# A GRU with 16 experts behind it: new states by one scan over pairs, 1 - z on GpSimd, fewer experts inside the recurrence

## The reference

```python
def cell(h, x):
    gi = x @ W_ih + b_ih
    gh = h @ W_hh + b_hh
    r = sigmoid(i_r + h_r)
    z = sigmoid(i_z + h_z)
    n = tanh(i_n + r * h_n)
    return (1.0 - z) * n + z * h          # the new state
S = softmax(xf @ router_w + router_b)     # xf: the 4096 states, 16 experts
G, idx = top_k(S.T, 256)
out = xf[idx] @ expert_w + expert_b
y[idx] += G * out
result = x + y
```

## Time and profile before

| | |
|---|---|
| time, median of 3 | 1116.22 us (1114.98 to 1118.48) |
| profiled execution | 1120.15 us, span 1118.0 us |
| TensorE busy | 1099.6 us, 98% of the span |
| VectorE busy | 836.9 us, 75% |
| ScalarE busy | 407.2 us, 36% |
| GpSimd busy | 7.0 us, 1% |
| mean granted TensorE clock | 0.995 |
| chain that ended last | TensorE 94%, VectorE 3%, DMA 1%, no named cause 1% |

### The profile page before, as it was taken

One profiled execution on the slowest core, in us unless ns is written; L12 is line 12 of the kernel. 1 busy time (PEld: TensorE's weight loads), 2 busy tenths in 40 slices (PEclk: granted clock), 3 DMA queues, 4 the chain that ended last, 5 costly groups with the idle time before them and its releaser, 6 DMA issues.

```text
span 1118.0 us, 61876 instructions
## 1 busy us (share of the span) xinstructions
PE 1099.6 (98%) x27307; PEld 904.6 (81%) x27307; DVE 836.9 (75%) x4504; ACT 407.2 (36%) x1618; POOL 7.0 (1%) x31
## 2 busy tenths in 40 slices
PE   8999999999999999999999999999999999999898
PEld 5778888888888888888888888888888888888772
DVE  5777777777777777777777777777777777776786
ACT  2333333343333333333433433333433334333340
POOL 2000000000000000000000000000000000000000
PEclk9999999999999999999999999999999999999999
DMA  6311111001111111001100000000000000001318
GB/s 250 88 22 22 23 22 23 12 15 21 22 23 22 23 22 23 7 19 22 23 13 14 13 13 13 8 9 13 13 13 13 13 13 4 4 3 52 87 31 274
DMA packets 80258, 36.85 MB, mean 33 GB/s; under 512 B 69987, under 2 KB 69987, under 8 KB 79990
## 3 DMA queue, kind: packets, MB, share of 16 engines
q1 hardware_dynamic: 77648, 28.66, 10.7%
q10 hardware_dynamic: 2342, 4.24, 1.1%
HBM read 24.49 MB, written 8.39 MB: 29 GB/s over the span
## 4 chain that ended last, share of the span: by engine, by line
PE 94%; DVE 3%; DMA 1%; issue 1%; SPq 0%; ACT 0%; DVEq 0%
PE gates L567 59%; PE gates L504 25%; PE ffn_ps L610 5%; PE gates L610 4%; DMA whh<-in_L_cond_W_hh 1%; PE log_ps L619 1%; DVE wih L908 0%; DVE u L794 0%; PE log_ps L691 0%; SPq L275 0%; ACT th L396 0%; DVE zT L801 0%; DVE tok L819 0%; SPq L278 0%; DVE z_h L806 0%
## 5 line engine op out<-in xcount | busy, mean ns | idle before, releaser
L567 PE MATMUL gates<-whh,tok 128*16 128x192 f32 x16384 | 714.0, 326 | 4.9 <-DVE tok L819 2.5
L567 PEld LDWEIGHTS gates<-whh,tok 128*16 128x16 f32 x16384 | 558.9, 124 | 111.2 <-DVE tok L819 4.6
L396 ACT ACTIVATE th<-gates 128x128 f32<-128x128 f32 x512 | 140.2, 274 | 340.9 <-PE gates L567 340.9
L794 DVE SCALAR_TENSOR_TENSOR u<-th,gates 128x64 f32<-128x64 f32 x512 | 113.4, 221 | 198.8 <-ACT th L396 198.8
L401 ACT ACTIVATE n_t<-v 128x64 f32<-128x64 f32 x512 | 131.6, 257 | 277.5 <-DVE v L798 277.5
L504 PE MATMUL gates<-wih,xS 128*32 128x192 f32 x3024 | 146.0, 326 | 0.0
L810 DVE STREAM_TRANSPOSE nT<-n_t 128x64 f32<-128x64 f32 x512 | 123.7, 242 | 0.0
L801 DVE STREAM_TRANSPOSE zT<-th 128x64 f32<-128x64 f32 x512 | 121.5, 237 | 0.0
L798 DVE SCALAR_TENSOR_TENSOR v<-u,gates 128x64 f32<-128x64 f32 x512 | 112.9, 221 | 8.8
L504 PEld LDWEIGHTS gates<-wih,xS 128*32 128x32 f32 x3024 | 98.3, 110 | 22.8
L819 DVE SCALAR_TENSOR_TENSOR tok<-new_n,z_h 128x32 f32<-128x32 f32 x512 | 109.8, 214 | 8.7
(11 more groups left out here) (134 smaller groups left out, 526.8 us busy)
## 6 DMA issues: line engine op xcount, KB each, us to landing
x_in<-in_x SPq DMA_DIRECT2D x248, 32.0 KB, 2.1
xs<-in_x SPq DMA_DIRECT2D x18, 256.0 KB, 3.6
out<-tok SPq DMA_DIRECT2D x16, 256.0 KB, 3.8
out<-tok ACTq DMA_DIRECT2D x16, 256.0 KB, 3.8
wih<-in_L_cond_W_ih SPq DMA_DIRECT2D x4, 768.0 KB, 7.2
whh<-in_L_cond_W_hh SPq DMA_DIRECT2D x4, 768.0 KB, 13.7
whh<-in_x SPq DMA_DIRECT2D x12, 256.0 KB, 5.9
we<-in_L_ffn_expert_w SPq DMA_DIRECT2D x1, 1024.0 KB, 5.2
```

What stands on the lines that cost most here:

```text
L396: nc.scalar.activation(th[a][:, :, :].rearrange("p g c -> p (g c)"), gates[t // S % PAIRS][a][:, R_:HN], ACT.Tanh, scale=0.5).then_inc(th_ ...
L567: mm = nc.tensor.matmul(gates[t // S % PAIRS][a][Q * j:Q * j + rows, R_:GC].rearrange("b (g k c) -> b g k c", g=G, k=KH), columns, by_tile ...
L794: V.scalar_tensor_tensor(u[a][:, :], th[a][:, 0, :], 1.0, ps[a][:, HN:GC], ALU.add, ALU.mult).then_inc(u_ready[a], 1)
```

## The change

VectorE no longer makes new_n and the new state by two instructions in each half. GpSimd makes 0.5 - 0.5 * zT into every second element of `away`; the elements between are 0 for good. `nT` now holds pairs: n from the transpose, and z_h beside it. One scan with multiply and add over the 64 elements of `away` and `nT` (state = away * previous + nT) then gives n at the first of each pair (away is 0 there) and away * n + z_h at the second, which is the new state. States live in a ring of two steps, `states`, from which TensorE takes its columns with a stride of two, and GpSimd copies each into its token tile. half_h is made in two halves. The experts start at step 118, with seven tiles in the loop. Rounds hold ten units, short ones six. Of the 512 units 132 instead of 212 are done by the end of the loop, and 334 instead of 391 when the weights have been gathered; 16 tiles instead of 11 are output from PSUM. `we` is loaded in four pieces at steps 4 to 7, and of the 14 late loads all but the first wait for a search round each.

```diff
-    PAD = P
-    IN_LOOP = 12
+    IN_LOOP = 7
-    FIRST = 18
+    FIRST = 118
-    LAST_UNITS, SOFTMAX_UNITS, ROUND_UNITS, SHORT_UNITS = [3, 6, 6, 6], 28, 9, 4
+    LAST_UNITS, SOFTMAX_UNITS, ROUND_UNITS, SHORT_UNITS = [3, 6, 6, 6], 28, 10, 6
-    PSUM_PLACES = [0, 1, 2, 3, 4, 9, 14, 18, 22, 27, 31]
+    PSUM_PLACES = [0, 1, 2, 3, 5, 7, 10, 12, 14, 17, 19, 21, 24, 26, 28, 31]
...
+        away = [sb(f"away{a}", [P, KH, B, 2]) for a in range(2)]
+        nT = [sb(f"nT{a}", [P, S, KH, B, 2]) for a in range(2)]
+        states = [sb(f"states{a}", [P, (1 + S * KH) * B * 2]) for a in range(2)]
+        state = [states[a][:, B * 2:].rearrange("p (s k b two) -> p s k b two", s=S, k=KH, two=2) for a in range(2)]
...
-            sp.dma_start(we[:, :, :], expert_w.rearrange("(k p) d -> p k d", p=P)).then_inc(ffn_w_loaded, 16)
...
                 load_x(n)
+                if n == 2:
+                    for k in range(K):
+                        sp.wait_ge(h_ready[1], 4 + k)
+                        sp.dma_start(we[:, k, :], expert_w[k * P:(k + 1) * P, :]).then_inc(ffn_w_loaded, 16)
...
             for n in range(XS, NT):
+                if n > XS:
+                    sp.wait_ge(cnt_all, n - XS)
                 load_xs(n)
...
+            for t in range(T):
+                for a in range(2):
+                    pool.wait_ge(zT_ready[a], t + 1)
+                    if t:
+                        pool.wait_ge(h_ready[a], t)
+                    nc.gpsimd.tensor_scalar(away[a][:, :, :, 1], zT[a][:, :, rows], -0.5, 0.5, ALU.mult, ALU.add)\
+                        .then_inc(away_ready[a], 1)
+                for a in range(2):
+                    pool.wait_ge(h_ready[a], t + 1)
+                    nc.gpsimd.tensor_copy(by_chunk[:, a * KH:(a + 1) * KH], state[a][:, (t + 1) % S, :, :, 1]).then_inc(h_kept[a], 1)
...
-                    end = PAD + (t - 1) // TT * D + (kc + 1) * P
-                    columns = tok[:, end - rows * TT + (t - 1) % TT:end:TT]
+                    end = (1 + s * KH + kc % KH + 1) * B * 2
+                    columns = states[kc // KH][:, end - rows * 2 + 1:end:2]
...
-                def take_n(a):
-                    dve.wait_ge(nT_ready[a], t + 1)
-                    V.scalar_tensor_tensor(new_n[a][:, :, :], zT[a][:, :, rows], 1.0, nT[a][:, :, rows],
-                                           ALU.subtract, ALU.mult).then_inc(new_n_ready[a], 1)
...
+                def new_state(a):
+                    dve.wait_ge(nT_ready[a], t + 1)
+                    dve.wait_ge(z_h_ready[a], t + 1)
+                    dve.wait_ge(away_ready[a], t + 1)
+                    if t >= S:
+                        dve.wait_ge(h_kept[a], t - S + 1)
+                    V.tensor_tensor_scan(state[a][:, (t + 1) % S, :, :, :].rearrange("p k b two -> p (k b two)"),
+                                         away[a][:, :, :, :].rearrange("p k b two -> p (k b two)"),
+                                         nT[a][:, s, :, :, :].rearrange("p k b two -> p (k b two)"), 0.0, ALU.mult,
+                                         ALU.add).then_inc(h_ready[a], 1)
```

More of the change, by code:

```diff
@@ L108, in gru_expert_choice_kernel @@
         p7 = sb("p7", [P, HN])
-        tok = sb("tok", [P, PAD + NT * D])
+        tok = sb("tok", [P, NT * D])
         half_h = sb("half_h", [P, K, B])
@@ L117, in gru_expert_choice_kernel @@
         zT = [sb(f"zT{a}", [P, KH, Q]) for a in range(2)]
-        nT = [sb(f"nT{a}", [P, KH, Q]) for a in range(2)]
-        z_h = [sb(f"z_h{a}", [P, KH, B]) for a in range(2)]
-        new_n = [sb(f"new_n{a}", [P, KH, B]) for a in range(2)]
+        away = [sb(f"away{a}", [P, KH, B, 2]) for a in range(2)]
+        nT = [sb(f"nT{a}", [P, S, KH, B, 2]) for a in range(2)]
+        states = [sb(f"states{a}", [P, (1 + S * KH) * B * 2]) for a in range(2)]
+        state = [states[a][:, B * 2:].rearrange("p (s k b two) -> p s k b two", s=S, k=KH, two=2) for a in range(2)]
         def tile(n):
-            return tok[:, PAD + n * D:PAD + (n + 1) * D]
+            return tok[:, n * D:(n + 1) * D]
         x_first = tile(NT - 2)
@@ L131, in gru_expert_choice_kernel @@
         ones = tile(NT - 4)[0:1, P:P + Q]
-        bih, bhh = (tok[0:1, PAD + n * D:PAD + (n + G) * D].rearrange("p (g c) -> p g c", g=G) for n in (NT - 8, NT - 12))
+        bih, bhh = (tok[0:1, n * D:(n + G) * D].rearrange("p (g c) -> p g c", g=G) for n in (NT - 8, NT - 12))
         xs = sb("xs", [P, XS, D])
@@ L234, in gru_expert_choice_kernel @@
         nT_ready = [sem(f"nT_ready{a}") for a in range(2)]
-        new_n_ready = [sem(f"new_n_ready{a}") for a in range(2)]
+        z_h_ready = [sem(f"z_h_ready{a}") for a in range(2)]
+        away_ready = [sem(f"away_ready{a}") for a in range(2)]
+        h_kept = [sem(f"h_kept{a}") for a in range(2)]
         h_ready = [sem(f"h_ready{a}") for a in range(2)]
@@ L330, in _ @@
                                     channel_multiplier=1).then_inc(ident_ready, 1)
-            nc.gpsimd.memset(tok[:, 0:PAD], 0.0).then_inc(pad_cleared, 1)
+            for a in range(2):
+                nc.gpsimd.memset(away[a][:, :, :, :], 0.0)
+                nc.gpsimd.memset(states[a][:, :], 0.0).then_inc(pairs_cleared, 1)
             then_step(nc.gpsimd.memset(same_expert[:, :], 0.0))
@@ L349, in _ @@
                                     fill=0.0, base=NE - 1, channel_multiplier=-1).then_inc(masks_ready, 1)
+            for t in range(T):
+                rows = slice(t % S * B, (t % S + 1) * B)
+                by_chunk = tile(t // TT).rearrange("p (k b t) -> p k b t", k=K, t=TT)[:, :, :, t % TT]
+                for a in range(2):
[4 more added lines that the diff above has]
+                        .then_inc(away_ready[a], 1)
+                for a in range(2):
+                    pool.wait_ge(h_ready[a], t + 1)
+                    nc.gpsimd.tensor_copy(by_chunk[:, a * KH:(a + 1) * KH], state[a][:, (t + 1) % S, :, :, 1]).then_inc(h_kept[a], 1)
         @block.scalar
@@ L608, in expert @@
                         pe.wait_ge(ffn_preset, n + 1)
+                        pe.wait_ge(h_kept[1], (n + 1) * TT)
                     for j in range(J):
@@ L617, in router @@
                 for kc in range(K):
+                    if quad == NT // QUAD - 1 and kc % KH == 0:
+                        pe.wait_ge(h_kept[kc // KH], T)
                     for j in range(J):
@@ L674, in _ @@
                         pe.wait_ge(log_biased, 1)
+                    pe.wait_ge(h_kept[1], t)
                     router(t // (QUAD * TT) - 1)
@@ L788, in step @@
                 ps = gates[t // S % PAIRS]
-                by_chunk = tile(t // TT).rearrange("p (k b t) -> p k b t", k=K, t=TT)[:, :, :, t % TT]
                 chunks = [slice(a * KH, (a + 1) * KH) for a in range(2)]
@@ L833, in step @@
                 turn_n(1)
-                take_n(1)
                 new_state(1)
-                dve.wait_ge(h_ready[1], t + 1)
-                V.tensor_scalar(half_h[:, :, :], by_chunk, 0.5, None, ALU.mult).then_inc(half_h_ready, 1)
+                for a in range(2):
+                    dve.wait_ge(h_ready[a], t + 1)
+                    V.tensor_scalar(half_h[:, chunks[a], :], state[a][:, (t + 1) % S, :, :, 1], 0.5, None, ALU.mult)\
+                        .then_inc(half_h_ready, 1)
             for t in range(T):
@@ L841, in _ @@
                 step(t)
-                if t == TT:
+                if t == 2 * TT:
                     dve.wait_ge(ffn_w_loaded, FFN_LOADS)
```

21 lines of the change are left out of this document (8 added, 13 removed).

## The result

The changed kernel takes **1125.49 us**, median of four runs (1124.05 to 1126.57), beside 1116.85 (1114.98 to 1118.48) for the kernel before on the same chip: a ratio of 1.0069 [1.0054, 1.0085], **0.7% slower**. The forecast was 1117.1 in a range of 1110 to 1130, with 0.38 for "the same" and 0.38 for "slower". The profiled execution took 1126.57 us with a span of 1124.6, 6.6 more than the span of 1118.0 before.

What follows compares the result with a forecast made beforehand. It took TensorE and the state's dependence loop to bound steps equally at 3.90 us, TensorE mostly afterwards. Terms summed to +0.9 on the profiled 1120.15 us, giving 1121.1; less 3.9 to the median, 1117.1 us, range 1110 to 1130.

Steps and rivals of the forecast that it cites:

- third steps shorter, four-unit steps gone: Loop before step 118: 29 steps without expert work gain 0.15 us each, five four-unit steps give back 1.0; together -5.4 us.
- steps from 118 on: Loop from step 118: portions are the old ones and TensorE fills most steps, so no gain, 0.
- `we` in four: Early loop: cutting the 1 MB `we` load in four removes an unnamed TensorE wait of 0.83 us; -0.8 us.
- tenth unit in rounds: Search rounds: a tenth expert unit in fourteen rounds, partly covered by some 0.13 us TensorE slack; +1.2 us (0 to 3.0).
- late loads: Search: one x load per round removes TensorE's 3.07 us standstill and 1.7 us of lower clock; -4.8 us (0 to -4.8).
- more units last: Last phase: 14 more groups of 512 columns and one single unit, which nothing hides; +12.3 us.
- wait and clock ahead of the last experts: Before the weights' matmuls: three more units fill half of TensorE's 1.18 us wait, clock drop open; -0.9 us (0 to -1.7).
- end: Kernel end: with stores spread over a longer phase, the last store has less queue in front; -0.7 us (0 to -1.5).
- third rival: TensorE's standstills stay or move if they come from the program's own length: 1122.7 us, 0.6% slower; chance 0.11.
- A path shortened by 0.15 us: New state path in each step: the scan replaces new_n and tok, with GpSimd's work barely hidden; bound 0.18 us if wholly hidden.
- First rival: State path: GpSimd is late, each 0.1 us beyond some 0.7 from zT costs 25.6 us; 1147 us, chance 0.23.
- Second rival: Full loop steps partly wait for the state, so all 256 steps shorten by 0.03 us: 1109.4 us; chance 0.22.

Runs made afterwards that it cites:

- experiment 3: The kernel before with only its loads spread, `we` in four pieces and the late x loads a round apart: 1112.38 us, ratio 0.9949.
- experiment 2: The kernel before with only the new schedule of experts, states and loads as before: 1129.6 us, ratio 1.0099.
- 10: The kernel before with only the 14 late x loads spread, `we` still loaded in one piece: 1115.19 us, ratio 0.9968.
- experiment 1: The changed kernel (scan, GpSimd, loads spread) with the old schedule of experts: 1113.95 us, ratio 0.9951.
- 5 to 10: Changed kernel with copies held back, one or two extra GpSimd instructions, nine/four units, earlier second v; then old kernel, x loads spread: 1126.03, 1187.45, 1275.63, 1125.95, 1141.32, 1115.19 us.
- experiment 4: The changed kernel with all 14 late loads issued at once behind the last step, as before: 1126.11 us, ratio 1.0057.
- experiment 5: The changed kernel with GpSimd's first copy also waiting for the second half's state: 1126.03 us, ratio 1.0068.

## Why the prediction was off by 8 us, step by step

The time lies in the range, but the likeliest case, no change within 0.3%, was not what happened. Of the 8.4 us between 1117.1 and 1125.49, 5.5 are the terms (the profiled execution came at 1126.57, not 1121.1), and 2.8 the offset to the median, which was 3.9 in the trace of before and is 1.1 now. The offset isn't mere chance: the profiled execution of before had the lower clock in two places, 1.7 us each, and by their mean clocks many other executions of that kernel had less of it (experiment 3). The prediction took 1.7 us and more for the clock off the profiled time, and then the whole 3.9 as well, which counts in part the same thing twice. The terms, in us of the profiled span:

| step | forecast | measured | from |
|---|---|---|---|
| third steps shorter, four-unit steps gone | -5.4 | -3.6 | steps 18 to 118: -3.3, of which -1.5 also with the old path (experiment 2); -0.3 ahead of them |
| steps from 118 on | 0 | +1.2 | starts of steps 118 and 253; single late scans |
| `we` in four | -0.8 | -1.5 | experiments 3 and 10 |
| last router, softmax | 0 | -0.1 | to first count |
| tenth unit in rounds | +1.2 | +2.7 | 14 x (2.43 - 2.24) |
| short rounds | 0 | +0.2 | 2 x (1.56 - 1.48) |
| late loads | -4.8 | -1.6 | over need: 6.0 to 4.4 |
| more units last | +12.3 | +12.2 | 39.4 against 27.2 in experiments 1 and 3 |
| wait and clock ahead of the last experts | -0.9 | -1.8 | 10.5 less 12.2, and 0.1 of the wait |
| end | -0.7 | -1.0 | tail |
| **sum** | **+0.9** | **+6.7** | spans: +6.6 |

**Where it failed.** The step that failed most is "the late loads: -4.8". It tied the standstill to the DMA burst, and that held: no kernel with spread loads has one above 1.13 us (1, 3, 5 to 10 and the changed one), and every kernel with the burst does (before, 2, 4). That it is instructions arriving late was only argued there, and the instruction packets of the traces bear it out (experiment 4). But its size was taken from a trace of nine-unit rounds and added to a change that also makes them ten. Experiments 3 and 4 separate the two: -4.4 us in the old schedule, 0 in the new one. The third rival (the standstills move) was therefore right for this kernel, for 3.2 of its 5.6 us, and had been given 0.11. Its reason, the program's own length, was not: with the loads over early the same program has no small standstills. Why rounds of ten units lose more to the spread loads (2.4 to 4.4 us) than rounds of nine (1.5 to 2.4) is open.

**The loop** gave -2.4 instead of -5.4. "A path shortened by 0.15 us" was true of the first half alone (0.14). The second half came 0.07 sooner, and in a short step TensorE needs it 24 records on, so it became the limit: 0.10 a pair. The cause is a sum: GpSimd's turn was put at 0.40 of 0.48 free us and is 0.51, so the second scan starts 0.10 us later against the tanh than new_n did (2.53 instead of 2.43), which leaves 0.07 of the 0.17 that the shorter work gives. From step 118 on the single late scans of experiment 1 cost 1.2, the term that I had at 0.

**The tenth unit** cost 0.19 of its 0.217 us in each round; the "slack of 0.13 us" was not slack. The bound of 3.0 was right and the value chosen wrong: a record count times a rate from another stage is no measure of idle time.

**The last phase** was right to 0.1 us: units of the same size at a rate read from the same stage. Only against the kernel before it shows as 10.5, since that one had lost 1.7 to the clock.

**First rival.** GpSimd was not late, but its price and margin were both wrong. The prediction gave it up to some 0.7 us from zT. From zT's end at 502.64 to the scan's start at 503.15 it takes 0.51, of which 0.20 is the way back to VectorE, and there is no slack towards the scan and about 0.1 us in the whole step: I had counted the slack of the last consumer, TensorE, and not the chain through VectorE's queue between. And each 0.1 us costs 51 us, not 25.6, as it is paid in both halves. **Second rival**: refuted, full steps stay at 3.90 us.

**A slip in the working.** The lower bound of the loop term is 29 x 0.18 + 1.0, that is -6.2 and not -6.3. It changes nothing.

## What to carry to other kernels

- Work taken out of an inner loop isn't gained there if the loop's own dependence is as long as its work. Find both lengths first; here they were 3.90 and 3.90, and 25 lighter steps gave 3.3 us where the moved units cost 12.2 at the end.
- When an operation goes over to another engine, count the handovers (here 0.06 to 0.09 us there and 0.20 back) and count how often in a step the detour is paid: two halves in one queue pay it twice.
- Test a change's parts alone: the best version here is the old kernel with the spread loads only, 0.5% faster, and the full change hides it behind +12 us.

## What the runs showed of the hardware

- A small GpSimd tensor_scalar or copy (128 x 32, f32) takes 0.23 to 0.25 us, 0.17 to 0.18 back to back. It starts 0.06 to 0.09 us behind the end of the VectorE instruction it waits for; VectorE then starts 0.20 us behind its end.
- No contention between GpSimd and VectorE was seen: z_h takes 0.194 us with `away` beside it, and 0.193 before without; the scan starts at the same distance with and without GpSimd's copy beside it (experiment 5). The rule of the Trainium skill, SBUF — State Buffer, section Who interferes with whom, is that a VectorE instruction with two SBUF inputs contends with a GpSimd instruction that reads SBUF, since its second input comes through the shared read interface; it is not seen at this size.
- TensorE can stand still for 0.3 to 1.1 us, with nothing released by a semaphore, at a DMA share of only 0.35 (here with ten units a round), where 0.91 brought 2.4 to 3.1 us. All 32 such standstills of this case end 1.24 to 1.72 us behind the landing of a 16 KB packet of the queue `instruction`.
- The granted clock was 0.63 over 4.6 us behind each standstill of 2.4 to 3.1 us (before, experiments 2 and 4), and 1.00 over the whole search of the changed kernel, whose longest is 1.13 us. Executions of one program differ in it: 0.992 to 0.998 on average for the kernel before, with 7 us between the fastest and the slowest.
